# Activation tiles turned by DMA instead of by TensorE, and a new order of the second layer's steps

## The reference, cut to what matters

```
x = x + xattn0(layernorm(x), ctx)      # 32 heads of 128, 8 key-value heads
x = x + ffn0(layernorm(x))             # relu^2 up/down + fc1, expert, fc2 scaled by the top-2 gate sum; layernorm
x = x + xattn1(rmsnorm(layernorm(x)), ctx)   # 32 heads of 16, 8 key-value heads, softmax over 64 keys
x = x + ffn1(layernorm(x))             # logits = x@W_gate + b; for 8 experts relu(x@W_e + b_e); mean of the top two
```

## Time and profile before

| | us |
|---|---|
| median of 3 runs | 1830.26 |
| lowest, highest | 1821.8, 1833.26 |
| the profiled execution | 1821.84 |
| its span | 1820.0 |
| PE busy | 1711.9 (94%) |
| DVE busy | 1226.9 (67%) |
| ACT busy | 758.5 (42%) |
| POOL busy | 485.7 (27%) |

### The profile page before, as it was taken

How to read it: one execution, slowest core, us unless ns; L and a number is a source line. 1 busy time by engine, 2 the same in 40 slices (tenths; PEclk the granted TensorE clock), 3 DMA queues, 4 the chain that set the end, 5 groups by cost and what they waited for, 6 DMA issues and landing times.

```text
span 1820.0 us, 32614 instructions
## 1 busy us (share of the span) xinstructions
PE 1711.9 (94%) x12832; PEld 907.5 (50%) x12832; DVE 1226.9 (67%) x2352; ACT 758.5 (42%) x1335; POOL 485.7 (27%) x370
## 2 busy tenths in 40 slices
PE   5889999999999999999998999998899999999997
PEld 2445555555555555555554444444454444444443
DVE  5776656655665656465657577776878878877863
ACT  5443333333333333333334333343555555545542
POOL 0152650704407025066000000000122322322324
PEclk9899999999999999999999999999999999999999
DMA  6122241412404114035311300002433333333230
GB/s 237 36 59 70 76 145 24 160 27 59 128 13 139 50 45 146 18 93 174 93 37 24 122 1 1 1 1 105 150 71 65 58 65 64 59 65 64 57 66 12
DMA packets 188976, 131.08 MB, mean 72 GB/s; under 512 B 172832, under 2 KB 173088, under 8 KB 180896
## 3 DMA queue, kind: packets, MB, share of 16 engines
q1 hardware_dynamic: 121248, 112.28, 21.4%
q10 hardware_dynamic: 67584, 16.79, 5.3%
HBM read 65.60 MB, written 20.97 MB: 48 GB/s over the span
## 4 chain that ended last, share of the span: by engine, by line
PE 64%; DVE 17%; DMA 7%; ACT 7%; issue 5%; DVEq 0%; ACTq 0%; POOL 0%; SPq 0%; POOLq 0%
PE bank L716 59%; DMA R<-R 7%; PE bank L762 3%; DVE R L1995 2%; DVE smx L1983 2%; ACT R L1430 2%; ACT R L1187 1%; DVE smx L1973 1%; DVE smx L1643 1%; PE bank L658 1%; PE bank L1010 1%; DVE R L1827 1%; ACT R L1338 1%; DVE AW L1645 1%; DVE bank L1977 1%
## 5 line engine op out<-in xcount | busy, mean ns | idle before, releaser
L716 PE MATMUL bank<-R 128*128 128x512 f16 (+1 forms) x7152 | 1298.9, 341 | 22.5 <-DVE R L1590 7.0
L716 PEld LDWEIGHTS bank<-R 128*128 128x128 f16 x7152 | 583.9, 98 | 666.4 <-issue 34.0
L1590 DVE SCALAR_TENSOR_TENSOR R<-bank,biases,R 128x512 f16<-128x512 f32 x288 | 204.7, 746 | 218.7 <-ACT R L1179 176.0
L578 POOL TENSOR_TENSOR R<-R 128x512 f32<-128x512 f32 x112 | 145.3, 1297 | 409.3 <-ACT R L1389 408.0
L1179 ACT ACTIVATE R<-bank,biases 128x512 f16<-128x512 f32 x128 | 87.7, 686 | 255.3 <-PE bank L716 254.5
L469 POOL TENSOR_SCALAR R<-R 128x2048 f32<-128x2048 f32 (+1 forms) x20 | 32.9, 1646 | 416.3 <-PE bank L716 351.5
L1389 ACT ACTIVATE R<-R,msk 128x512 f32<-128x512 f32 x128 | 90.5, 720 | 61.3 <-DVE R L1941 60.7
L716 PE MATMUL bank<-CT,R 128*128 128x512 f16 x384 | 94.2, 398 | 22.9 <-DVE CT L1564 11.5
L1602 DVE SCALAR_TENSOR_TENSOR R<-bank,R 64x512 f16<-64x512 f32 x64 | 44.0, 688 | 98.8 <-ACT R L1187 98.4
L1675 DVE SCALAR_TENSOR_TENSOR X<-bank,X 128x512 f32<-128x512 f32 x128 | 86.8, 683 | 32.2 <-PE bank L716 32.1
L1941 DVE SCALAR_TENSOR_TENSOR R<-bank,R 128x512 f32<-128x512 f32 x128 | 87.0, 680 | 21.4 <-PE bank L716 20.2
(11 more groups left out here) (156 smaller groups left out, 1724.3 us busy)
## 6 DMA issues: line engine op xcount, KB each, us to landing
R<-in_wB SPq DMA_DIRECT2D x16, 1024.0 KB, 5.6
R<-in_wX SPq DMA_DIRECT2D x16, 1024.0 KB, 4.8
w_split<-AW SPq DMA_DIRECT2D x16, 1024.0 KB, 4.9
R<-w_split SPq DMA_DIRECT2D x12, 1024.0 KB, 6.9
R<-in_ctxT SPq DMA_DIRECT2D x4, 1024.0 KB, 9.8
X<-in_x SPq DMA_DIRECT2D x4, 1024.0 KB, 13.6
out<-X SPq DMA_DIRECT2D x16, 256.0 KB, 2.0
R<-in_wB SPq DMA_DIRECT2D x7, 512.0 KB, 5.6
```

Of the source, the lines that this page charges most:

```text
L578: g.tensor_tensor(acc, acc, tmp[:, e % 2, :], ALU.add).then_inc(e_acc, 1)
L716: last = pe.matmul(dst, a(sa), b(sb_), start=(k == 0), stop=(k == m - 1))
L1590: v.scalar_tensor_tensor(out=dst, in0=src, scalar=bias, in1=hi, op0=ALU.add, op1=ALU.subtract).then_inc(done, 1)
```

## The change

Four things, all after stage B.

1. In FFN chunks 0 to 2, SP turns the four tiles by DMA straight into `T1` (once the chunk's 12 jobs are done). Two more `xs` slots (`room`) let all four tiles be split without waiting for a turn. PE waits for four semaphores `fx_in` at the end of the chunk. The third tile's normalisation moves ahead of DVE's first `y_of`.
2. In layer 1, steps 2 to 15, both `tile_turn`s and both `tile_store`s go; SP issues `turn_ffn` (to `T2`) and `turn_attn` (to a buffer of its own, `TA`).
3. PE's order: `project(n+1)` now comes ahead of the gate, and `scores(n+1,0)` ahead of `output(n)` (which writes bank 7 now, not 0); e5 goes to the start of the next step.
4. The orders of DVE and ACT follow: `less_max(n+1,0)` and its exponentials end the step ahead of `add_out(n)`; e4's bias is taken after `add_out`, e5's at the start of the next step; `q_lo` and `kv_lo` come before `out_scale(n,0)`. Odd tiles have a `V` of their own, and queries of tiles from 3 on lie in a part of `CT`.

Step 1 (`step_one`) keeps its PE turns, but has `scores(2,0)` before `output(1)`. A few semaphores of weight loads are merged.

```diff
 # SP
+            for c in range(NC - 1):
+                sp.wait_ge(u_mm, 12 * (c + 1))
+                for t in range(TC):
+                    sp.wait_ge(n_lo, chunk_first(c) + t + 1)
+                    sp.dma_start_transpose(T1[:, :, :, t * P:(t + 1) * P].rearrange("p s k n -> p (s k) n"),
+                                           room(t).rearrange("p s d -> p (s d)")).then_inc(fx_in[t], 16)
...
+            def turn_norm(n, sem_, par, dst):
+                sp.dma_start_transpose(dst.rearrange("p s k n -> p (s k) n"),
+                                       xs[:, par].rearrange("p s d -> p (s d)")).then_inc(sem_, 16)
+            def turn_ffn(n):
+                sp.wait_ge(n_lo, ffn_stat(n) + 1)
+                if n == 1:
+                    sp.wait_ge(a_kv, 3)
+                else:
+                    sp.wait_ge(e_mm, (n - 1) * NE)
+                turn_norm(n, fn_in, 0, T2[n % 2])
+            def turn_attn(n):
+                sp.wait_ge(n_lo, attn_stat(n) + 1)
+                sp.wait_ge(a_kv, n)
+                sp.wait_ge(b_plo, 4)
+                turn_norm(n, an_in, 1, TA)
...
             turn_k(2)
+            turn_attn(3)
             for n in range(2, NT):
+                turn_ffn(n - 1)
                 turn_p(n, 0)
                 store_out(n - 2)
                 turn_p(n, 1)
                 if n < NT - 1:
                     turn_q(n + 1)
                     turn_k(n + 1)
+                if n < NT - 2:
+                    turn_attn(n + 2)
+            turn_ffn(NT - 1)
 # PE, FFN chunk
-                    if t < 2:
-                        for u in (2 * t, 2 * t + 1):
-                            tile_turn(pe, n + u, u % 2, 4 + u % 2, n + (u - 1))
-                pe.wait_ge(n_stored, n + TC)
+                for landed in fx_in:
+                    pe.wait_ge(landed, (c + 1) * 16)
 # PE, layer 1
-                    pe.wait_ge(e_bias, n * NE + e - 1 if e > 0 else n * NE)
+                    pe.wait_ge(e_bias, n * NE + e - 1)
...
+            def attn_step(n, ctx_t):
+                more = n < NT - 1
+                last, this = T2[n % 2], T2[1 - n % 2]
+                expert(n - 2, 5, last)
+                expert(n - 2, 6, last)
+                scores(n, 1)
+                expert(n - 2, 7, last)
                 if more:
+                    project(n + 1, ctx_t, TA)
+                gate(n - 1, this)
+                expert(n - 1, 0, this)
                 weigh_v(n, 0)
+                expert(n - 1, 1, this)
+                expert(n - 1, 2, this)
+                weigh_v(n, 1)
+                expert(n - 1, 3, this)
+                pe.wait_ge(r_lg, n)
+                turn_o(n)
+                expert(n - 1, 4, this)
                 if more:
+                    scores(n + 1, 0)
                 output(n)
 # DVE, layer 1 (new order)
+            def add_and_mean(n):
+                add_out(n)
+                expert(n - 1, 4)
+            def attn_step(n, odd):
+                more, norm = has(n, -1), has(n, -2)
+                expert(n - 2, 5)
+                norm_apply(dve, ffn_stat(n - 1), 0, x_tile(n - 1), yn)
+                row_sums(n, 0)
+                ffn_lo(n - 1)
+                reciprocals(n, 0)
+                probs_lo(n, 0)
+                expert(n - 2, 6)
+                expert(n - 2, 7)
+                less_max(n, 1)
+                mask_of(n - 1)
+                row_sums(n, 1)
+                probs_lo(n, 1)
+                expert(n - 1, 0)
+                if more:
                     q_lo(n + 1)
+                    kv_lo(n + 1, not odd)
+                out_scale(n, 0)
+                out_lo(n, 0)
+                reciprocals(n, 1)
+                expert(n - 1, 1)
+                if norm:
+                    norm_stats(dve, attn_stat(n + 2), 1, x_tile(n + 2), True)
+                expert(n - 1, 2)
+                out_scale(n, 1)
+                out_lo(n, 1)
+                if norm:
+                    norm_apply(dve, attn_stat(n + 2), 1, x_tile(n + 2), yn)
+                    tile_lo(dve, attn_stat(n + 2), 1, yn, 0)
+                expert(n - 1, 3)
                 if more:
+                    less_max(n + 1, 0)
+                add_and_mean(n)
 # ACT, layer 1 (new order)
+            def attn_step(n):
+                more, norm = n < NT - 1, n < NT - 2
+                norm_hi(n - 1)
+                for e in (5, 6, 7):
+                    expert(n - 2, e)
                 exponentials(n, 1)
                 if more:
+                    project_hi(n + 1)
+                expert(n - 1, 0)
                 out_hi(n, 0)
+                expert(n - 1, 1)
...
+                    exponentials(n + 1, 0)
```

More of the change, by code:

```diff
@@ L1039, in expert, with step_one @@
                 if not (isinstance(n, int) and n == 0 and e < 2):
-                    pe.wait_ge(e_bias, n * NE + e - 1 if e > 0 else n * NE)
+                    pe.wait_ge(e_bias, n * NE + e - 1)
                 group3(banks[2 + e % 2], [(lambda p, k=k: tt[:, p, k, :], lambda p, k=k: We[e][:, p, k, :])
                                           for k in range(KC)], e_mm)
[L1045 to L1060, removed]
+            def step_one(ctx_t):
+                n = 1
+                pe.wait_ge(f_y, NT - 1)
+                tile_turn(pe, ffn_stat(0), 0, 7, ffn_turn(0))
+                turn_p(n, 0)
+                gate(0, T2[0])
+                expert(0, 0, T2[0])
+                pe.wait_ge(r_lg, n)
+                tile_turn(pe, attn_stat(2), 1, 7, attn_turn(2))
+                weigh_v(n, 0)
+                expert(0, 1, T2[0])
+                turn_p(n, 1)
+                project(2, ctx_t, T2[1])
+                weigh_v(n, 1)
+                expert(0, 2, T2[0])
+                turn_o(n)
+                expert(0, 3, T2[0])
+                expert(0, 4, T2[0])
+                scores(2, 0)
+                output(n)
@@ L1064, in attn_step @@
                 weigh_v(n, 0)
[L1065 to L1068, removed]
-                if more:
[L1070 to L1078, removed]
@@ L1079, in attn_step @@
-                turn_o(n)
-                if one:
-                    expert(n - 1, 3 if more else 4, T2[1 - buf])
+                expert(n - 1, 1, this)
+                expert(n - 1, 2, this)
+                weigh_v(n, 1)
+                expert(n - 1, 3, this)
+                pe.wait_ge(r_lg, n)
+                turn_o(n)
+                expert(n - 1, 4, this)
+                if more:
+                    scores(n + 1, 0)
                 output(n)
-                if more:
-                    expert(n - 1, 4, T2[1 - buf])
-                    scores(n + 1, 0)
@@ L2052, in attn_step @@
                 reciprocals(n, 1)
-                if one:
-                    expert(n - 1, 1)
-                if not two:
-                    y_norm(NT - 1)
-                    y_add_to_x(NT - 1)
-                if has(n, -2):
-                    norm_stats(dve, attn_stat(n + 2), 1, x_tile(n + 2), True)
+                expert(0, 1)
+                y_norm(NT - 1)
+                y_add_to_x(NT - 1)
+                norm_stats(dve, attn_stat(n + 2), 1, x_tile(n + 2), True)
                 out_scale(n, 1)
```

288 lines of the change are left out of this document (143 added, 145 removed).

## The result

The changed kernel took 1805.29 us (median of 4, 1803.51 to 1806.0) against 1828.72 us for the kernel before (median of 4): ratio 0.9885, 95% interval 0.9861 to 0.9908. That is 23 us by the medians and 21 by the ratio; the forecast was 1793, and the measured time lies in the stated range.

The account below looks back on a forecast made before the run. PE was taken as the bound. Thirteen steps of layer 1 (29 us), the chunks (5), step 1 (0.7) and the end (0.2) gave 35 us off 1821.8 profiled, forecast as a median of 1793 us, range 1772 to 1814.

Parts of the forecast that it names:

- e5: Layer 1, an expert's piece on PE at the start of the new step, ahead of e6; done at 2.6 us.
- e4: Layer 1, an expert's piece: DVE's bias empties its bank at 3.0 us, where PE comes at 2.6 for e6.
- the new step of layer 1: Layer 1, scores to scores: 31.4 us forecast, bounds 30.5 and 32.7; gain 2.25 us a step, 29 us over thirteen.
- So PE sets the pace, and a gain has to take work or waits off PE: Layer 1: PE, busy 412 of 438 us, was taken as what bounds the kernel.
- POOL's meetings with DVE: Layer 1, Newton's step for the FFN beside POOL's add of e4: 0.2 us a step taken of a 1.1 us delay.
- The layout's waits: PE's waits per new step: e6 0.4 us, `weigh_v(n,1)` 0.4, `turn_o` 0 to 0.1; gate, `weigh_v(n,0)` and `scores(n+1,0)` none.
- e6: Layer 1, an expert's piece on PE after e5: waits 0.4 us a step for DVE to empty e4's bank.
- e2: Layer 1, an expert's piece: a wait of 0.4 us forecast in the last stretch, from `scores(15,0)` on.
- the floor of the forecast: Layer 1 step with no waits, PE's bare work: 30.5 us; as a rival, 1771 to 1779 us, chance 0.1.
- Landings: DMA transposes in layer 1: 3.7 us for the new turns, 4.2 for `turn_p`; longest seen before 5.9.
- The rival "slower": Layer 1: transfers crowd each other and landings double; step about 36 us, time some 1850 us; chance 0.05.
- The rival "DVE becomes the bound": Layer 1: DVE, 85% busy, delayed by ACT and POOL, closes at 32.5 to 33 us; 1803 to 1816 us; chance 0.18.

Follow-up runs that it names:

- dma_old_order: Kernel before, with the FFN chunks' turns and both turns of steps 2 to 15 by DMA, PE, ACT and DVE in old order; 1822.35 us, ratio 0.9974.
- bias_first: relus_late with e4's bias on DVE ahead of the residual add instead of behind it; 1783.83 us, ratio 0.9769, and again 1787.86 us, ratio 0.9778.
- pool_narrow: Changed kernel with POOL adding only 8 of 512 columns, so most of the experts' sum is left out; 1783.96 us, ratio 0.9771.
- relus_late: Changed kernel with ACT taking out_hi of batch 1 ahead of e2's relu and the FFN input's high part ahead of e4's relu; 1787.16 us, ratio 0.9783.
- output_first: relus_late with the next tile's first scores behind this tile's output, and e4's bias behind the maxima on DVE; 1832.41 us, ratio 1.0038.
- relu_after_hi: Changed kernel with only one ACT move, out_hi of batch 1 ahead of e2's relu; 1790.92 us, ratio 0.9812.
- bias_first_fill: bias_first with the norm of tile n+2 between DVE's out_scale and out_lo, and ACT's high part moved with it; 1789.6 us, ratio 0.9798.
- output_first_b: bias_first with the next tile's first scores behind the output on PE; DVE: e4's bias, residual add, maxima; ACT: root before exponentials; 1810.84 us, ratio 0.9919.

## Why the prediction came out as it did

The time lay in the range; the likeliest value was 12 us too low. The step of the sum that failed is the new step of layer 1: 31.4 us forecast, with bounds of 30.5 and 32.7, and 32.73 measured in an undisturbed step, at the upper bound. Over the thirteen steps 16.7 us of the 29 came, so 12.3 are missing. (13 times 1.33 would be 17; but the trace before had 4.9 us more than thirteen undisturbed steps, most of it in two that took 35.0 and 37.0 us, and that came back as gain.) The other terms came to 5.9 us, as forecast: chunks 6.0, step 1 0.2, from `scores(15,0)` to the end -0.3, where 5, 0.7 and 0.2 were forecast.

- **"So PE sets the pace, and a gain has to take work or waits off PE": wrong.** dma_old_order took the turns of steps 2 to 15 off PE and the step stayed. The step was a chain of 14.0 us from scores to `weigh_v`, its first part DVE's queue, and 19.7 us of PE's queue behind it. The rows for it were in my hands: the earlier trace rows has both starts, and the waits for landings in the earlier trace rows, 20 in some twelve steps, say that the chain is late in most. I read 94% busy as a bound. The gain came only with the new order: it holds more work between the scores and `weigh_v` (18.95 us from 1504.83 to 1523.78, with no wait for the landing). No run has the new order with the turns left on PE, so how much of the gain the moved turns give once the order is there isn't shown. By an estimate they take 0.9 us of PE a step (0.45 each) and PE's floor would be 31.4 us with them; bias_first, at 31.3, lies just under that. I had priced the moves as the frame in which the turns' time is saved; the time came out near because the layout by hand followed every engine and so had the chain in it.
- **POOL's meetings with DVE: the mis-sized term.** I had seen one in the earlier trace rows, took 0.2 us of 1.1 and put it at Newton's step for the FFN. There were two on the cycle, that one and `out_lo`, each 0.94 us. Moving ACT's relus, which times POOL, took the step from 32.58 to 31.45 in the column and from 32.7 to 31.4 undisturbed: the whole of the miss. pool_narrow, with ACT's order untouched, gives the same 31.44.
- **The layout's waits.** e6 0.4: measured 0.40. `weigh_v(n,1)` 0.4: 0.17. The gate and `weigh_v(n,0)` none: none. `turn_o` 0 to 0.1: 0.77, for an `out_lo` that POOL held. (ACT took e2's relu ahead of `out_hi`, so that DVE waited 0.76 for it and not 0.48; in pool_narrow that stays and PE's wait is gone.) `project` 0.27 was not in the layout: it needs `probs_lo(n,0)`. Counted between starts, where an expert takes 2.59 us, the four waits cost 0.56, 0.45, 0.33 and 0.93 us at e6, `project`, `weigh_v(n,1)` and `turn_o`, 2.27 in all; 32.73 less 2.27 is 30.5, the floor of the forecast. So PE's bare work was priced right and the waits, 0.9 with POOL's 0.2, were not. (The recorded sum is 31.4 before it is rounded down to 31.2, and has 0.2 for POOL on top.) With the relus moved the step is the 31.4 of the forecast: the waits at e6 and `weigh_v(n,1)` are left, 0.89 us over the floor. That it agrees so closely is in part luck, as the forecast came there with a rounding and with 0.2 for POOL.
- **Landings.** I took 3.7 and 4.2 us and feared up to 5.9. The two new turns, then `turn_p`:

```profile
L459 SPq DMA_TRANSPOSE R<-R x28: 1231/1232/1254, 1305.5 to 1772.1; - x28
...
DMA to landing us min/median/max: 3.0/3.3/4.8
...
L456 SPq DMA_TRANSPOSE R<-R x28: 1317/1904/2716, 1320.7 to 1752.9; - x28
...
DMA to landing us min/median/max: 4.3/4.4/5.3
```

  A tile has seven transposes after five (the prediction's eight and six are miscounted), and the medians of `turn_p` and `turn_q` rose by 0.2 us, to 4.4. The sign of being wrong that did show is a landing over 5 us: 5.3 at most for `turn_p`, 6.2 for `turn_q`; but the longest before were 5.9 and 5.8. The rival "slower", and the estimate from the Trainium skill's page (VectorE: DVE Perf Modes, The three transpose paths) of 10.5 us for eight blocks, fall with these rows.
- **The chunks.** 5 us forecast, 6.0 measured, with landings (3.2 us) hidden as said.
- **Step 1 and the end.** `scores(2,0)` did wait for `turn_k(2)` (2.54 us), as said; the stretch up to it is 0.2 us shorter where 0.7 was forecast. The gate of tile 14 waited 2.01 us, forecast 2.0. The rest, 64.9 us before, was 62.2: 0.2 was forecast from scores to the first expert of tile 15, and it was 1775.61 - 1732.52 = 43.09 after 42.76 in the earlier trace rows; the 2.7 of the column lie ahead of its other end, as it starts at `scores(15,1)`, behind the output that the new order moved.

```profile
1307.21 0.61 PE L1031 MATMUL bank<-R 48*128 48x64 f16 x16 [2.54 <-DMA R<-R]
...
1746.21 0.46 PE L763 MATMUL bank<-g1w,R 128*128 128x8 f16 x12 [2.01 <-DMA R<-R]
...
1775.61 20.88 PE L763 MATMUL bank<-R 128*128 128x512 f16 x96
```

- **The rival "DVE becomes the bound"** was given 0.18 and 1803 to 1816; that is what happened: 32.73 a step and 1805. Its reason was half right. DVE's sum of work fits (bias_first does the same work at 31.3); what it lacked was the time in which POOL held it.

## What to carry to other kernels

An engine that is busy 94% of the time need not be the bound: measure the distance between two events of the chain in the trace and look which engine is busy along it, and if taking work out from between them would leave only a wait, move work into that stretch rather than off the engine. When DVE and POOL both read two SBUF tensors, lay their operations out against each other; which instruction ACT takes first decides when POOL starts. Compare stretches between fixed events, since an unchanged stage ahead of the change can shift by more than the change is worth.

The fastest version here is bias_first (1783.83 and 1787.86 us, ratio 0.9769 and 0.9778), with relus_late (1787.16) inside its spread: 17 to 21 us under the changed kernel by medians, from three moves in ACT's and DVE's order.

## What the runs showed of the hardware

A DVE operation of 128x1 values takes 0.16 us alone and 1.10 when a POOL add of 1.26 us began 0.18 us before it; it ends 0.02 us after the add.

The granted clock fell to half (1.2 GHz) for 3.4 or 6.8 us at a time, 4 to 11 times in each trace after its first 200 us (the last of them cut short by the end in most), at places that all kernels share (once between 991 and 1005 us and once between 1227 and 1251 us in every trace) and at others that come and go between executions of one kernel (between 851 and 862 us: not in the first trace of before, 3.4 us at 858 in the second). In output_first, where PE paused 2.4 us in most steps, there were six such stretches from 1305 to 1630 us, within layer 1's steps, and a mean clock of 0.980; in bias_first, with pauses of at most 1.4, none between 1287 and 1778 us, and 0.988. That pauses bring them on is suggested by this and not shown; against it, in bias_first PE had paused 3.4 us ahead of 854.7 us and the clock stayed full.

The spread of 10 us in stage B falls in two groups. In the ten traces whose first `ffn_down` came at 1043.7 us or later, DVE kept PE waiting 2.5 to 3.4 us near 852 us; in the four where it came at 1038.6 to 1040.3 (the first of before, relu_after_hi, bias_first_fill, output_first_b) it didn't. The same kernel shows both; what decides it stays open.
